# The order of ACT's work in the output phase of a cross-attention kernel: the last two norms of a unit placed behind the exponentials of the next

## The reference

```
attn = (q @ Wq + bq) . (ctx @ Wk + bk)        per head, 1024 x 64
attn = attn * mask; attn = attn - max(attn)   one maximum over everything
attn = exp(attn) * mask
attn = attn / (sum(attn, axis=-1) + 1e-15)
out  = (attn . (ctx @ Wv + bv)) @ Wo + bo
y = out + x
result = (y - mean(y)) / sqrt(var(y) + 1e-5) * gamma + beta
```

## Time and profile before

| | |
|---|---|
| median of 3 runs | 1738.48 us (1737.42 to 1738.65) |
| the profiled execution | 1738.39 us |
| its span, first to last instruction | 1736.5 us |
| mean granted TensorE clock | 0.982 |
| busy: PE / DVE / ACT / POOL | 93% / 66% / 54% / 31% of the span |
| DMA | 382 MB, mean 220 GB/s |

### The profile page before, as it was taken

The page is one execution under the profiler, slowest core; times in us unless marked ns, Lnnn a source line. Parts: engine busy times, 40 slices in busy tenths (PEclk is TensorE's granted clock), DMA queues, the critical chain, the costliest instruction groups (busy, mean ns, idle before and its releaser), DMA issues. The chain is left out here.

```text
span 1736.5 us, 30465 instructions
## 1 busy us (share of the span) xinstructions
PE 1619.3 (93%) x10501; PEld 796.7 (46%) x10501; DVE 1151.8 (66%) x2138; ACT 935.5 (54%) x1383; POOL 544.1 (31%) x778
## 2 busy tenths in 40 slices
PE   4999999999999999999983999999999999999997
PEld 4445555455554555545531344444444444444443
DVE  6666555565556655566542777878778787878774
ACT  6755555555555555555534555555555555555542
POOL 0000000000000000000000567677666767677677
PEclk8999999999999999999995999999999999999999
DMA  6463444534445444453327999999999999999971
GB/s 231 146 226 121 164 176 151 222 122 160 172 157 217 127 154 172 163 211 128 153 97 247 265 308 314 290 286 292 313 318 295 291 313 316 278 293 297 310 234 73
DMA packets 92556, 382.11 MB, mean 220 GB/s; under 512 B 7520, under 2 KB 12768, under 8 KB 74592
## 3 DMA queue, kind: packets, MB, share of 16 engines
q1 hardware_dynamic: 92512, 381.53, 65.7%
HBM read 250.43 MB, written 131.07 MB: 220 GB/s over the span
## 5 line engine op out<-in xcount | busy, mean ns | idle before, releaser
L78 PE MATMUL ps_o<-u,p_hi 128*128 128x512 f16 x1024 | 389.7, 381 | 5.0 <-DVE p_lo L985 5.0
L69 PE MATMUL ps_s<-x_hi,g_hi 128*128 128x512 f16 x1024 | 389.1, 380 | 3.7 <-ACT s L496 3.7
L79 PE MATMUL ps_o<-u,p_hi 128*128 128x512 f16 x1024 | 389.4, 380 | 0.0
L80 PE MATMUL ps_o<-u,p_lo 128*128 128x512 f16 x1024 | 389.2, 380 | 0.0
L71 PE MATMUL ps_s<-x_hi,g_lo 128*128 128x512 f16 x1024 | 388.8, 380 | 0.0
L70 PE MATMUL ps_s<-x_lo,g_hi 128*128 128x512 f16 x1024 | 388.6, 380 | 0.0
L496 ACT ACTIVATE s<-ps_s,c_bias 128x512 f32<-128x512 f32 x256 | 176.1, 688 | 314.1 <-PE ps_s L71 311.0
L1052 POOL MEMSET zeros<- 128x256 f32 x1 | 0.3, 311 | 905.9 <-POOLq L138 905.9
L985 DVE TENSOR_TENSOR p_lo<-ps_p,p_hi 128x512 f16<-128x512 f32 x256 | 175.4, 685 | 126.3 <-ACT p_hi L902 126.0
L616 DVE TENSOR_TENSOR score_max<-score_max,tile_max 128x1 f32<-128x1 f32 x257 | 40.7, 158 | 310.5 <-ACT s L496 308.8
L912 ACT ACTIVATE y<-y,shift,rstd 128x512 f32<-128x512 f32 x128 | 104.1, 813 | 243.4 <-POOL shift L1073 238.9
(11 more groups left out here) (90 smaller groups left out, 2363.1 us busy)
## 6 DMA issues: line engine op xcount, KB each, us to landing
r_bc<-reciprocals SPq DMA_DIRECT2D x128, 512.0 KB, 8.1
scores<-s SPq DMA_DIRECT2D x30, 2048.0 KB, 7.6
x<-xT_in SPq DMA_DIRECT2D x32, 1024.0 KB, 9.5
u_halves<-u_out SPq DMA_DIRECT2D x64, 512.0 KB, 3.2
s_more<-scores SPq DMA_DIRECT2D x16, 2048.0 KB, 16.3
u<-u_halves SPq DMA_DIRECT2D x16, 2048.0 KB, 22.3
y<-x_in SPq DMA_DIRECT2D x32, 1024.0 KB, 18.1
out<-y SPq DMA_DIRECT2D x31, 1024.0 KB, 12.3
```

Source lines behind the costliest of these rows:

```text
L69: pe.matmul(out, lhs_hi, rhs_hi, start=first, stop=False)
L78: pe.matmul(out, lhs_hi, rhs_hi, start=False, stop=False, skip_group_check=True)
L79: pe.matmul(out, lhs_hi, rhs_lo, start=False, stop=False, skip_group_check=True)
L80: return pe.matmul(out, lhs_lo, rhs_hi, start=False, stop=False, skip_group_check=True)
```

## The change

ACT's order within a unit is written anew. The exponentials of unit n + 3 stand in the first third, one after half 1 and one after half 2; norms 2 and 3 of unit n are taken out of unit n and stand in unit n + 1, norm 2 behind the first exponential and norm 3 behind the second and half 3 (`behind`); the fill of bank 3 for unit n moves from the end of unit n - 1 to behind half 0 of unit n. The first unit has no norms behind it, and the last unit's norms 2 and 3 are issued at the end. The first group is split off the loop, because its first unit differs. The other engines' programs are the same.

```diff
-            def group(g, last):
+            def group(g, first, last):
                 for u in range(UNITS):
                     n, s = g * UNITS + u, (u + 1) % 2
                     more, more3 = not (last and u == UNITS - 1), not (last and u >= UNITS - 3)
                     halves = lambda *ps: [round_p(n + 1, s, p) for p in ps] if more else None
-                    halves(0, 1)
+                    behind = lambda t: None if first and u == 0 else norm(g if u else g - 1, (u - 1) % UNITS, t)
                     if more3:
                         tiny(n + 3)
+                    halves(0)
+                    fill(n, 3)
+                    halves(1)
+                    if more3:
                         exps(n + 3, u + 3, 0)
-                    halves(2, 3)
+                    behind(2)
+                    halves(2)
+                    if more3:
+                        exps(n + 3, u + 3, 1)
+                    halves(3)
+                    behind(3)
                     if more:
                         fill(n + 1, 0)
+                    halves(4, 5)
                     norm(g, u, 0)
-                    if more3:
-                        exps(n + 3, u + 3, 1)
-                    halves(4, 5)
                     if more:
                         fill(n + 1, 1)
+                    halves(6, 7)
                     norm(g, u, 1)
-                    halves(6, 7)
                     if more:
                         fill(n + 1, 2)
-                    norm(g, u, 2)
-                    if more:
-                        fill(n + 1, 3)
-                    norm(g, u, 3)
+                if last:
+                    norm(g, UNITS - 1, 2)
+                    norm(g, UNITS - 1, 3)
...
-            for t in range(TB):
+            for t in range(TB - 1):
                 fill(0, t)
...
-            with act.Fori(0, NG - 1) as g:
-                group(g, False)
-            group(NG - 1, True)
+            group(0, True, False)
+            with act.Fori(1, NG - 1) as g:
+                group(g, False, False)
+            group(NG - 1, False, True)
```

## The result

The changed kernel takes 1747.58 us (1746.21 to 1748.93), the kernel before, beside it on the same chip, 1738.48 us (1737.42 to 1739.21). The ratio is 1.0052, with a 95% interval of 1.0037 to 1.0067: slower by half a per cent. Forecast were 1745.0 and slower. The profiled execution took 1746.21 us and its span is 1744.3 us, 7.8 us longer than before.

The account below looks back on a forecast made before the run. The DMA queue, at 24.52 us a unit against the engines' 24.37, was taken as the bound. Unit 31's first exponential at 1647.3 to 1648.5, plus 95.2 to the end, plus 1.9, gave 1745.0 us; range 1738 to 1757.

Parts of the forecast that it names:

- The queue is the pacemaker: In the output phase the DMA queue needs 24.52 us a unit, slower than the engines' 24.37, and sets the pace.
- No gain from the removed waits: Removing ACT's 4.07 us wait per unit and PE's 1.6 us, at face value 46 us, was put at nothing.
- The engines' new ring is as long as the old one: Engines' cycle from one unit's first exponential to the next: 24.2 to 24.9 us, POOL's tiles replacing ACT's wait.
- A: Start of a unit's first exponential on ACT; for unit 31 forecast at 1647.3 to 1648.5 us, 1644.94 before.
- The hole of the y store: SP's y store waits for POOL's last beta, so the queue runs dry: 3.1 us lost once, in the first units.
- The queue's own pace of 24.52: Time per unit between landings of scores, 24 units apart in the kernel before: 24.52 us.
- The tail: From unit 31's first exponential to the end, set by POOL's 15 tiles: 95.2 us, against 91.6 before.
- Longer ring: Rival: the engines' cycle per unit exceeds 24.52 us, giving 1754 or about 1765 us; chance 0.17.
- Paced by the queue, no hole: Rival: the queue sets the pace and loses nothing at the y store; 1741.3 us, the same; chance 0.18.
- Faster, small: Rival: POOL's tiles come at 5.0 us or less, so POOL catches up; 1731 to 1738 us; chance 0.11.
- Faster, the full aim: Rival: PE's wait goes and the queue keeps up at 45.3 us a pair of units; 1692 us; chance 0.03.
- two signs that I named as refuting the forecast: Units below 24 us, or SP no longer waiting for its stored reciprocals: the queue was never at its own pace.

Follow-up runs that it names:

- f_after: The changed kernel with SP's load of scores issued one unit earlier, between the store of the reciprocals and their spread; 1719.14 us, ratio 0.9871.
- l_after: The changed kernel with fewer bytes of x and u loaded from the second group on (wrong output, timing only); 1710.88 us, ratio 0.9842.
- f_before: The kernel before with SP's load of scores issued between the store of the reciprocals and their spread; 1738.21 us, ratio 1.0001.
- l_before: The kernel before with fewer bytes of x and u loaded from the second group on (wrong output, timing only); 1738.98 us, ratio 1.0004.
- h_after: The changed kernel with SP's y store moved behind the loads, ahead of the store of the reciprocals; 1745.31 us, ratio 1.0042.
- qv_after: The changed kernel with a load of scores before the spread, norm 2 before the first exponential, and half the spread issued by ACT; 1711.14 us, ratio 0.984.

## Why the prediction was right, and where its terms were off

**The queue is the pacemaker: right.** It rested on 24.52 us a unit for the queue against 24.37 for the engines. That is a small difference, and the whole case hung on it. The changed kernel's exponentials start on their landing in every second unit, the share stays at 0.94, and f_after and l_after gain 28 and 37 us where f_before and l_before gain nothing.

**No gain from the removed waits: right**, and for the reason given, the queue. But of PE's 49.1 us only 11.6 went; the other 37.5 stayed, behind exponentials that now waited for their scores.

**"The engines' new ring is as long as the old one", 24.2 to 24.9 us: wrong.** It is 23.1 to 23.5 us where nothing waits for the queue: 23.2 on average in l_after, 23.48 and 23.15 in the changed kernel's own first units, and 22.67 in a unit that follows a wait for scores. In the unit of l_after shown above, 23.52 us long, the walk can be checked. From A to half 6 I had 14.3 us, and it took 14.15 (1406.35 to 1420.50), so that part was nearly right: POOL's tiles came 5.22 and 5.80 us apart there, and I had taken 5.6. From half 6 to the first scaling I had 7.35, and it took 7.15 (to 1427.65). From there to the next A I had 2.5 to 3.2, and it took 2.22. In the changed kernel's unit behind a wait the same three are 13.72 (1057.18 to 1070.90), 6.71 (to 1077.61) and 2.24. The last term holds the lesson: for the scaling I allowed up to 0.7 us more beside POOL, because two of them take 2.74 us in the earlier trace rows, a place where DVE and POOL run into each other, and I moved that to a place where they no longer meet. The Trainium skill (SBUF — State Buffer, on engine ports) calls the shared port an exclusive lock; the two scalings of 1.31 us with no beta beside them, against 2.74 with one, agree with it. The rule was a reason for a shorter ring here as much as for a longer one, and I weighed it only one way. Because the queue hid the ring, the error did not reach the time; with room on the queue it turns the sign, as l_after shows: 28 us faster than l_before.

**The hole of the y store, 3.1 us once, then a slack of 0 to 1.2: right in kind, half in size.** The first landing on which an exponential waits moved from 1055.8 to 1057.2 us, 1.4 us later, and the windows at 995 to 997 us show a queue a third full, not empty. Moving the store (h_after) gave 2.3 us, which isn't clear of the noise.

**The queue's own pace of 24.52: the term that was off.** I took it over unchanged. It was 24.75, and 24 x 0.23 = 5.6 us. With the 1.4 us this is the whole of A's move, from 1644.2 to 1651.17 us; I had 1647.3 to 1648.5. h_after keeps this pace, so the place of the y store isn't its cause. What is remains open.

**The tail: right in kind, 2.1 us too long.** I had A + 95.2 and it was 1744.3 - 1651.17 = 93.1 us. Norm 0 came at A + 12.5 and not 13.1, and the 15 tiles took 1738.30 - 1663.65 = 74.65 us and not 76.1. The 6.0 us behind the last norm stood. Against the middle of my sum, 1743.1, A is 3.3 us later and the tail 2.1 shorter: 1744.3. Two of the terms erred in opposite directions, and the forecast owes some of its closeness to that.

**The rivals.** "Longer ring" fell: l_after shows 23.2. "Paced by the queue, no hole" gave 1741.3 us and missed by 6.3 where the forecast missed by 2.6; the hole of 1.4 us lies between its 0 and my 3.1. "Faster, small" came near its condition of tiles at 5.0 us or less: they came 4.91, 5.66 and 4.60 us apart in the unit at 1057.18 us. It still didn't come true, because scores come late when the exponentials come early. "Faster, the full aim" is what f_after and qv_after come towards, once SP's order is changed with ACT's. Of the two signs that I named as refuting the forecast, one stayed away: SP still waits for its reciprocals. The other, units below 24 us, did appear, in every second unit (22.67) and in the early ones. It refutes the engines' ring of 24.2 and not the queue's pace, since pairs still take 49.5 us; as I had put it, it couldn't tell the two apart. Of the signs for the forecast, the exponentials on their landing, the DMA share, the new waits of ACT (1.26, 2.32 and 2.29 us) and POOL without a wait for statistics came about as said; the y store waited in every unit, and the last exponential stood 87.1 us ahead of the last norm and not 89.

## What to carry to other kernels

When an engine's order is to be improved, take the pace of the DMA queue from its landings, 20 units or more apart, and hold it against the engines' pace: two rings within 1% of each other mean that shortening one of them can leave the other as the bound. Here the edit to the queue alone was worth nothing, the edit to ACT alone cost 9 us, and both together gained 19. Take an engine's ring from units that neither wait for the queue nor follow such a wait. Look for the cheap covers of a queue's hole (a load put between a small store and what waits for it) before looking for fewer bytes. And don't take a duration measured beside a contender into a place where the contender has gone.

## What the runs showed that was not expected

- A spread of 8 KB from DRAM over 64 partitions moves at 221 to 227 GB/s at a full DMA share, with elements of 8 KB or 2 KB and with its halves on one queue or on two. The Trainium skill (SBUF — State Buffer, on the DMA port swizzle) states that partitions 0 to 63 reach only half of the ports, so that such a transfer gets some 218 GB/s at most. The rate in the rows is close to that. The Trainium skill (SBUF — State Buffer, on issuing two DMAs to hit both halves) also states that two concurrent DMAs, one on a tile at partition 0 and one on a tile at partition 64, came to only 6% more than a single one; the windows of qv_after, at 221 GB/s, agree. This is a reason for the slow spread that needs no repeated rows of DRAM, and no run here decides between the two.
- The queue paced itself 0.23 us a unit more slowly in the changed kernel, with the same bytes, the same number of packets (92512) and about the same share.
- PE's new wait costs clock as well. Windows of the changed kernel:

```profile
1306.00:1308.00 2.00, 0.86 (x17) 0.42 (x16) 0.00 (x0) 2.00 (x3) 0.12 (x1) 1.00 0.29 108
1308.00:1310.00 2.00, 0.22 (x6) 0.00 (x0) 1.39 (x2) 2.00 (x2) 1.92 (x2) 1.00 0.90 242
1310.00:1312.00 2.00, 1.77 (x16) 0.59 (x16) 1.29 (x2) 0.75 (x3) 1.80 (x5) 0.50 0.99 217
1312.00:1314.00 2.00, 2.00 (x10) 0.76 (x7) 1.91 (x3) 1.73 (x3) 1.20 (x1) 0.65 0.99 213
1314.00:1316.00 2.00, 2.00 (x11) 0.91 (x10) 2.00 (x3) 0.60 (x1) 1.92 (x3) 1.00 1.05 225
```

  After PE had been busy for 1.08 of 4 us, the granted clock fell to 0.50, the level of 1.2 GHz, and was back at 1.00 by 1314 us. The mean of the run went from 0.982 to 0.972. Such a wait of PE is thus dearer than its own length. How much of the 9 us comes from the clock was not tried by itself.
